# Running the FFN's first matmul four blocks ahead of its second instead of one, in an eight-core transformer layer

## The chip, the cores and the metric

The kernel runs on one Trainium2 chip with 8 cores. Each core takes one batch element (4096 tokens of width 1024) and all weights, and works alone; the cores exchange nothing. The metric is the device time of one launch in microseconds (us), that of the slowest core.

## The reference, cut to what matters

One post-layernorm transformer layer in float32: causal attention with 16 heads of 64, then a feed-forward network (FFN) with 4096 hidden units. Both are followed by a residual add and a layernorm.

```python
def _L0_ffn_ref(x, w1, b1, w2, b2):
    h = jax.nn.gelu(jnp.einsum('bse,eh->bsh', x, w1) + b1, approximate=False)
    return jnp.einsum('bsh,he->bse', h, w2) + b2

x = L0_attn_hidden_states                       # (8, 4096, 1024)
x = _layernorm(x + _L0_attn_ref(x, ...), axis=-1)
x = _layernorm(x + _L0_ffn_ref(x, ...), axis=-1)
```

## The kernel before, in words

Every operation is entered once, in program order, with `sch.add` (or `sp_dma`, `gp_dma` for transfers) and the operations that it depends on. Each engine then runs its own operations strictly in the order in which they were entered, and waits on a semaphore for each dependency on another engine. So the order of the `sch.add` calls is the order of the work, per engine. A `sch.barrier()` separates three stages. Stage A is attention by pairs of heads, stage B is the output projection with the first layernorm, and stage C is the FFN with the second layernorm. The change lies in stage C, which begins at 2704 us of the profiled execution.

Stage C keeps w1 and w2 in SBUF as bf16. w1 was loaded in stage B; w2 comes in at the start of stage C in 32 transfers, one per block of hidden units, issued from GpSimd's queue with at most two under way. The tokens are cut into 16 groups of 256 (`NTGC`, `TGC`). For each group the kernel goes over 32 blocks of 128 hidden units, `hc`:

- F1 (line 1153): 8 matmuls of 128x256, which multiply w1 by the transposed tokens `x2Tt` into one PSUM bank. Banks 0 and 1 take turns.
- gelu (line 1175) on ScalarE, from that bank to a bf16 tile `htile`, of which there are two (`hb = hc % 2`).
- F2 (line 1190): 4 matmuls of 128x512, `htile` by w2, added up over all 32 blocks in banks 2 to 5. In the last block 4 more matmuls (line 1200) add the bias and close the sums.

F1 of block hc+1 is entered between the gelu and the F2 of block hc, so TensorE computes F1 one block ahead. At a group's end there is no next block in the loop (`f1_next = None`). What follows the last F2 is the group's layernorm, called the tail here: four VectorE adds of the residual, out of banks 2 to 5 (line 1219), two squares on ScalarE with a running sum (line 1236), small VectorE statistics (lines 1249 to 1285), Ln and Exp on ScalarE (1299, 1308), a small VectorE product (1317), two ScalarE passes that write the output (1329), and the store. Ln and gelu sit in different activation tables, so ScalarE loads a table ahead of Ln and another ahead of the next gelu. ScalarE's order is gelu 31 of group g, the tail of g, gelu 0 of group g+1.

The loads of a group (`x2Tt` in 8 transfers and the residual rows `x2t` in one, both double-buffered, SyncE's queue, line 229) are entered at the group's top. The `x2Tt` load waits until the last F2 of the group two earlier is done, the `x2t` load until that group's tail has read its buffer.

Of the kernel before, what the change touches and what calls it, by code (L numbers as in the profile page):

```python
# [7 lines left out]
F32 = mybir.dt.float32  # L8
BF16 = mybir.dt.bfloat16
AF = mybir.ActivationFunctionType  # L10
# [3 lines left out]
D = 1024  # L14
FF = 4096
NPAIR = 8
TGA = 512
TGC = 256
# [85 lines left out]
def build_nc(S=4096, debug_taps=False):  # L104
# [3 lines left out]
    NTGC = S // TGC  # L108

    nc = bass.Bass("TRN2", target_bir_lowering=False)  # L110
# [16 lines left out]
    r_d = nc.dram_tensor("r_s", [2, 1024], F32, kind="Internal").ap()  # L127
    if debug_taps:
        qkv_tap = nc.dram_tensor("qkv_tap", [3, 128, S], BF16, kind="ExternalOutput").ap()

    idf_d = nc.inline_tensor(np.eye(128, dtype=np.float32), "idf")
    idb_d = nc.inline_tensor(
# [14 lines left out]
    rowbf = nc.alloc_sbuf_tensor("rowbf", [128, 5632], BF16).ap()  # L147
# [5 lines left out]
    b1f = nc.alloc_sbuf_tensor("b1f", [128, 32], F32).ap()  # L153
# [10 lines left out]
    def bf(off, n):  # L164
        assert off + n <= AR_COLS, f"arena overflow {off}+{n} > {AR_COLS}"
        return AR[:, off : off + n]

    def f32v(off, n):
        assert off % 2 == 0 and off + 2 * n <= AR_COLS, f"arena f32 ovf {off}"
        return AR[:, off : off + 2 * n].bitcast(F32)  # L170
# [28 lines left out]
    C_w1 = 0  # L199
    C_w2 = C_w1 + 8 * FF  # L200
    C_h = C_w2 + 32 * 1024
    C_x2T = C_h + 2 * TGC
    C_x2 = C_x2T + 2 * 8 * TGC
    C_out = C_x2 + 2 * 4096
    C_scr = C_out + 2 * 4096
# [5 lines left out]
    def bank(i):  # L211
        return PS[:, 512 * i : 512 * i + 512]
# [4 lines left out]
    sch = Sched(nc)  # L217
    t = nc.tensor
    v = nc.vector
    sc = nc.scalar  # L220
# [3 lines left out]
    def sp_dma(stream, outs_ins, deps=(), tag=""):  # L224
        sem = sch._sem(stream)

        def em():
            for o, i in outs_ins:
                sp.dma_start(out=o, in_=i).then_inc(sem, 16)
        return sch.add("sp", em, deps, tag, n_dma=len(outs_ins), sem=stream)  # L230

    def gp_dma(stream, outs_ins, deps=(), tag=""):
        sem = sch._sem(stream)

        def em():
            for o, i in outs_ins:
                gp.dma_start(out=o, in_=i).then_inc(sem, 16)  # L237
        return sch.add("pool", em, deps, tag, n_dma=len(outs_ins), sem=stream)
# [39 lines left out]
    eb1 = sch.add("dve", lambda: v.tensor_copy(b1f, PS[0:128, 2048:2080]), (tb1,), "b1Tev")  # L278
# [307 lines left out]
    for tp_ in range(NTT // 2):  # L586
# [28 lines left out]
        ev = sch.add("dve", em_ev, (tr,), f"xTev{tp_}")  # L615
# [182 lines left out]
    w1sb = bf(B_w1, 8 * FF)  # L798
# [10 lines left out]
    for oc in range(8):  # L809
# [19 lines left out]
        ev = sch.add("dve", em_ev, (tr,), f"wpTev{oc}")  # L829
# [3 lines left out]
    w1_lds = []  # L833
# [19 lines left out]
    for g in range(NTG):  # L853
        sb_ = 48 * (g % 2)
# [22 lines left out]
        for tc in range(4):  # L877
            for oh in range(2):
                bki = (2 * tc + oh) % 2
# [23 lines left out]
                def em_y2(tc=tc, oh=oh, bki=bki, xtg=xtg, sb_=sb_, y2=y2):  # L903
# [9 lines left out]
                ev = sch.add(  # L913
                    "dve", em_y2, (mm, x_ld) + y2_readers_par[g % 2], f"y2{g}.{tc}.{oh}"
                )
# [103 lines left out]
        for tc in range(4):  # L1019
# [6 lines left out]
                    bias=stats[:, sb_ + 36 + tc : sb_ + 37 + tc],  # L1026
# [11 lines left out]
                    bias=stats[:, sb_ + 36 + tc : sb_ + 37 + tc],  # L1038
# [66 lines left out]
    w2sb = bf(C_w2, 32 * 1024)  # L1105
    sq_scrC = f32v(C_scr, 1024)
    w2_lds = []
# [6 lines left out]
        )  # L1114
        w2_lds.append(ld)

    h_user = [None, None]
    gelu_prev = [None, None]
    x2t_user = [None, None]
    x2_user = [(), ()]  # L1120
    out_store = [None, None]
    ffn2_bank_user = [None, None, None, None]
    prev_sqC = None
    for g in range(NTGC):
        gb = g % 2
        sb_ = 48 * gb
        x2Tt = bf(C_x2T + gb * 8 * TGC, 8 * TGC)
        x2t = f32v(C_x2 + gb * 4096, 2048)
        outt = f32v(C_out + gb * 4096, 2048)
        ld1 = sp_dma(  # L1130
            f"sa{g % 2}",
            [
                (x2Tt[:, TGC * fc : TGC * fc + TGC], x2T_d[fc][:, TGC * g : TGC * g + TGC])
                for fc in range(8)
# [1 line left out]
            (x2t_user[gb],),  # L1136
            f"cx2T{g}",
        )
        ld2 = sp_dma(
            f"sx{g % 2}",  # L1140
            [(
                x2t.rearrange("p (c f) -> p c f", c=2, f=1024),
                x2_d[TGC * g : TGC * g + TGC, :].rearrange("(c p) f -> p c f", p=128),
# [1 line left out]
            x2_user[gb],  # L1145
            f"cx2{g}",
        )
        def mk_f1(hc, x2Tt=x2Tt, g=g):
            hb = hc % 2
            def em_f1(hc=hc, hb=hb, x2Tt=x2Tt):  # L1150
                r = None
                for fc in range(8):
                    r = t.matmul(  # L1153
                        bank(hb)[:, 0:TGC],
                        w1sb[:, FF * fc + 128 * hc : FF * fc + 128 * hc + 128],
                        x2Tt[:, TGC * fc : TGC * fc + TGC],
                        start=(fc == 0),
                        stop=(fc == 7),
                    )
                return r  # L1160
            deps1 = [ld1, gelu_prev[hb]]
            if g == 0 and hc == 0:
                deps1 += w1_lds
            return sch.add("pe", em_f1, tuple(deps1), f"f1_{g}.{hc}")

        ffn2_first = True
        mm2 = None
        f1_next = mk_f1(0)
        for hc in range(32):
            hb = hc % 2  # L1170
            htile = bf(C_h + hb * TGC, TGC)
            mm1 = f1_next
            gl = sch.add(
                "act",
                lambda hc=hc, hb=hb, htile=htile: sc.activation(  # L1175
                    htile, bank(hb)[:, 0:TGC], AF.Gelu, bias=b1f[:, hc : hc + 1]
                ),
                (mm1, h_user[hb]) + ((eb1,) if g == 0 and hc == 0 else ()),
                f"gelu{g}.{hc}",
            )  # L1180
            gelu_prev[hb] = gl
            if hc < 31:
                f1_next = mk_f1(hc + 1)
            else:
                f1_next = None
            def em_f2(hc=hc, htile=htile, first=ffn2_first, last=(hc == 31)):
                r = None
                for tc in range(2):
                    for oh in range(2):
                        r = t.matmul(  # L1190
                            bank(2 + 2 * tc + oh),
                            htile[:, 128 * tc : 128 * tc + 128],
                            w2sb[:, 1024 * hc + 512 * oh : 1024 * hc + 512 * oh + 512],
                            start=first,
                            stop=False,
                        )
                if last:
                    for tc in range(2):
                        for oh in range(2):
                            r = t.matmul(  # L1200
                                bank(2 + 2 * tc + oh),
                                rowbf[0:1, 3072 : 3072 + 128],
                                rowbf[0:1, 4608 + 512 * oh : 4608 + 512 * oh + 512],
                                start=False,
                                stop=True,
                            )
                return r
            deps_f2 = [gl, w2_lds[hc]]
            if ffn2_first:
                deps_f2 += [d for d in ffn2_bank_user if d is not None]  # L1210
            mm2 = sch.add("pe", em_f2, tuple(deps_f2), f"f2_{g}.{hc}")
            h_user[hb] = mm2
            ffn2_first = False
        x2t_user[gb] = mm2
        ev_ops = []
        for tc in range(2):
            for oh in range(2):
                def em_y3(tc=tc, oh=oh, x2t=x2t, sb_=sb_):
                    return v.scalar_tensor_tensor(  # L1219
                        x2t[:, 1024 * tc + 512 * oh : 1024 * tc + 512 * oh + 512],  # L1220
                        bank(2 + 2 * tc + oh),
                        1.0,
                        x2t[:, 1024 * tc + 512 * oh : 1024 * tc + 512 * oh + 512],
                        ALU.mult,
                        ALU.add,
                        accum_out=stats[:, sb_ + 2 * tc + oh : sb_ + 2 * tc + oh + 1],
                    )
                ev = sch.add("dve", em_y3, (mm2, ld2), f"y3{g}.{tc}.{oh}")
                ffn2_bank_user[2 * tc + oh] = ev
                ev_ops.append(ev)  # L1230
        stat_ops = []
# [94 lines left out]
        for tc in range(2):  # L1326
# [6 lines left out]
                    bias=stats[:, sb_ + 36 + tc : sb_ + 37 + tc],  # L1333
# [4 lines left out]
            )  # L1338
            ap_ops.append(ap1)
        x2_user[gb] = tuple(ev_ops + sq_ops + ap_ops)  # L1340
        st = gp_dma(
            f"pa{g % 2}",
            [(
# [54 lines left out]
```

How the kernel before makes its waits and increments, by code:

```python
    def emit_engine(self, name, eng):  # L80
        sems = self.sems
        wm = {}
        for op in self.ops:
            if op.eng != name:
                continue
            for d in op.deps:
                if d.eng == "pe" and name == "pe":
                    continue
                v = d.val
                if wm.get(d.sem, 0) >= v:
                    continue
                eng.wait_ge(sems[d.sem], v)
                wm[d.sem] = v
            last = op.emit()
            if not op.is_dma:
                assert last is not None, f"op {op.tag} returned no instruction"
                last.then_inc(sems[op.sem], 1)
        if name == "pool":
            for sname, val in sorted(self.final.items()):
                if val > 0 and sname not in ("pe", "act", "dve"):
                    eng.wait_ge(sems[sname], val)
# [125 lines left out]
        def em():  # L227
            for o, i in outs_ins:
                sp.dma_start(out=o, in_=i).then_inc(sem, 16)
# [5 lines left out]
        def em():  # L235
            for o, i in outs_ins:
                gp.dma_start(out=o, in_=i).then_inc(sem, 16)
```

## Time and profile before

| what | value |
|---|---|
| time, median of 2 runs | 3853.24 us (3835.53 and 3870.95) |
| the profiled execution's own time | 3833.8 us |
| its span, slowest core (core 2) | 3832.3 us |
| spans of the 8 cores | 3810.2 to 3832.3 us |
| mean granted TensorE clock, every core | 0.886 to 0.892 |
| TensorE busy over the span | 2808.2 us (73%) |
| ScalarE busy over the span | 1722.7 us (45%) |
| first matmul of stage C | 2704.4 us |

The span is counted from the first to the last instruction of the core, and 1.5 us of the execution's time lie around it. TensorE is busy for three quarters of the span in the mean, but that is a mean of three stages with different limits, so the stage of the change has to be read by itself. "Granted clock" is the share of TensorE's 2.4 GHz that the chip let it have: rows show 1.00 or 0.50, and values between are means over a stretch that holds both. Some matmul records (a few per cent) are missing from the trace, so counts in it can be short by a few.

### The profile page before, as it was taken

How to read it: one execution, taken by the hardware profiler on the slowest of the kernel's cores; microseconds unless marked ns; L12 is line 12 of the kernel's file. 1: busy time of each engine (PE TensorE's matmuls, PEld its weight loads, DVE VectorE, ACT ScalarE, POOL GpSimd, SP SyncE). 2: the span in 40 equal slices, each digit the busy share in tenths (PEclk: the TensorE clock that was granted, in tenths of full speed). 3: DMA queues.
4: the chain of work that ended last, by engine and by line, in shares of the span. 5: the costliest groups of instructions: out<-in, count | busy, mean ns of one | idle time of the engine just before them, and what ended most of it. 6: DMA issues, size and time to landing. Idle time of an engine off the chain costs nothing.

```text
span 3832.3 us, 40822 instructions; the slowest of 8 cores (3810.2 to 3832.3 us)
## 1 busy us (share of the span) xinstructions
PE 2808.2 (73%) x14609; PEld 1235.5 (32%) x14609; DVE 1174.2 (31%) x2008; ACT 1722.7 (45%) x1969; POOL 337.7 (9%) x447
## 2 busy tenths in 40 slices
PE   5777667677668667677767675387678888788886
PEld 3421123121123121123221111132345555555554
DVE  3354353354353354353354343133000000000000
ACT  0036634736734736733736786145133333333333
POOL 1010100010100010100010111012200000000000
PEclk9889888989898988888979899688889989899898
DMA  5200000010100010100010000965720110101100
GB/s 78 34 9 9 25 6 12 6 28 6 28 6 12 6 28 6 28 6 12 6 28 6 23 12 13 189 224 198 149 60 28 34 50 28 56 28 34 50 28 23
DMA packets 71682, 154.55 MB, mean 40 GB/s; under 512 B 9760, under 2 KB 34496, under 8 KB 69440
## 3 DMA queue, kind: packets, MB, share of 16 engines
q0 software_dynamic: 34784, 100.96, 10.6%
q1 hardware_dynamic: 36704, 50.98, 4.6%
q8 instruction: 124, 2.03, 0.2%
q14 instruction: 70, 0.57, 0.1%
HBM read 134.88 MB, written 50.59 MB: 48 GB/s over the span
## 4 chain that ended last, share of the span: by engine, by line
PE 56%; ACT 14%; DVE 12%; DMA 9%; issue 8%; POOL 1%; DVEq 0%; ACTq 0%; SPq 0%; POOLq 0%
ACT arena L673 12%; PE ps L1190 11%; PE ps L1153 11%; PE ps L701 10%; PE ps L374 7%; PE ps L649 6%; PE ps L540 3%; PE ps L883 3%; DVE rowf L728 3%; DMA arena<-x 3%; DVE arena L682 2%; DMA arena<-w 2%; DVE rowf L727 2%; DMA arena<-wqkv 2%; PE ps L415 1%
## 5 line engine op out<-in xcount | busy, mean ns | idle before, releaser
L673 ACT ACTIVATE arena<-ps,cbt 128x1024 bf16<-128x1024 f32 x1152 | 1245.3, 1112 | 938.5 <-PE ps L649 932.0
L701 PE MATMUL ps<-arena 128*65 128x512 bf16 x2304 | 751.7, 410 | 327.5 <-DVE arena L682 157.3
L1190 PE MATMUL ps<-arena 128*128 128x512 bf16 x2048 | 539.0, 388 | 165.6 <-ACT arena L1175 146.7
L1153 PE MATMUL ps<-arena 128*128 128x256 bf16 x4096 | 543.5, 278 | 18.0 <-DMA arena<-x2T_s 18.0
L1175 ACT ACTIVATE arena<-ps,b1f 128x256 bf16<-128x256 f32 x512 | 240.5, 473 | 668.8 <-PE ps L1153 668.6
L649 PE MATMUL ps<-arena 64*128 64x512 bf16 x2304 | 474.5, 410 | 0.0
L1153 PEld LDWEIGHTS ps<-arena 128*128 128x128 bf16 x4096 | 406.3, 100 | 184.2 <-issue 33.8
L682 DVE TENSOR_TENSOR arena<-arena,masks_s 128x512 bf16<-128x512 bf16 x512 | 198.8, 430 | 639.2 <-ACT arena L673 638.7
L701 PEld LDWEIGHTS ps<-arena 128*65 128x65 bf16 x2304 | 170.5, 113 | 632.0 <-issue 621.5
L1219 DVE SCALAR_TENSOR_TENSOR arena<-ps,arena 128x512 f32<-128x512 f32 x64 | 40.4, 687 | 1026.5 <-PE ps L1200 1026.5
L1190 PEld LDWEIGHTS ps<-arena 128*128 128x128 bf16 x2048 | 199.8, 99 | 319.8 <-issue 191.8
L649 PEld LDWEIGHTS ps<-arena 64*128 64x128 bf16 x2304 | 111.1, 94 | 519.8 <-issue 519.7
L374 PE MATMUL ps<-arena 128*128 128x512 bf16 x1024 | 255.3, 394 | 23.2 <-DVE arena L609 11.8
L415 PE MATMUL ps<-arena,ones_bf 128*1 128x512 bf16 x128 | 57.9, 452 | 243.6 <-DVE arena L406 243.6
L727 DVE RECIPROCAL rowf<-arena 1x512 f32<-1x512 f32 x64 | 213.8, 3341 | 12.0 <-DVE arena L720 12.0
L728 DVE RECIPROCAL rowf<-arena 1x512 f32<-1x512 f32 x64 | 210.0, 3282 | 0.0
L883 PE MATMUL ps<-arena 128*128 128x512 bf16 x512 | 137.6, 417 | 61.0 <-DVE arena L904 60.1
L237 POOL DMA_DIRECT2D r_s<-rowf x64 | 34.7, 543 | 1658.5 <-DVE rowf L728 943.9
L395 DVE CAST arena<-ps 128x512 bf16<-128x512 f32 x128 | 88.5, 691 | 299.8 <-PE ps L381 299.7
L540 PE MATMUL ps<-arena 128*128 128x256 bf16 x1024 | 144.5, 288 | 14.6 <-DVE arena L568 13.6
L374 PEld LDWEIGHTS ps<-arena 128*128 128x128 bf16 x1024 | 93.4, 100 | 157.4 <-issue 73.6
L928 ACT ACTIVATE arena<-arena 128x1024 f32<-128x1024 f32 x32 | 33.8, 1056 | 189.0 <-PE ps L1066 107.6
(92 smaller groups left out, 1446.0 us busy)
## 6 DMA issues: line engine op xcount, KB each, us to landing
rb<-r_s POOLq DMA_DIRECT2D x64, 256.0 KB, 3.5
arena<-x SPq DMA_DIRECT2D x8, 2048.0 KB, 9.9
x_s<-arena POOLq DMA_DIRECT2D x8, 2048.0 KB, 7.4
arena<-x_s SPq DMA_DIRECT2D x16, 1024.0 KB, 6.2
out<-arena POOLq DMA_DIRECT2D x16, 1024.0 KB, 8.3
arena<-x POOLq DMA_DIRECT2D x16, 512.0 KB, 7.5
attn_s<-arena POOLq DMA_DIRECT2D x8, 1024.0 KB, 5.2
arena<-attn_s SPq DMA_DIRECT2D x64, 128.0 KB, 10.7
```

What stands on the lines that cost most here:

```text
L374: r = t.matmul(bank(bki), wT[:, 128 * fc : 128 * fc + 128], xTb[:, S * fc + TGA * g : S * fc + TGA * g + TGA], start=(fc == 0), stop=False,)
L540: r = t.matmul(bank(bki)[:, 0:256], xTb[:, S * fc + 128 * a : S * fc + 128 * a + 128], wvg[:, 256 * fc : 256 * fc + 256], start=(fc == 0), ...
L649: r = t.matmul(PS[:, 1024 * ub + 512 * hh : 1024 * ub + 512 * hh + 512], k2[64 * hh : 64 * hh + 64, 128 * j : 128 * j + 128], q2[64 * hh : ...
L673: return sc.activation(Pb, quad, AF.Exp, bias=cbcol, scale=0.125)
L682: r = v.tensor_tensor(Pb[:, 512 * hh : 512 * hh + 512], Pb[:, 512 * hh : 512 * hh + 512], masks[:, 512 * mi : 512 * mi + 512], ALU.mult,)
L701: r = t.matmul(PS[0:65, 3072 + 512 * hh : 3584 + 512 * hh], va[:, 65 * (NKT * hh + j) : 65 * (NKT * hh + j) + 65], Pb[:, 512 * hh : 512 * ...
L727: v.reciprocal(rowf[0:1, 0:512], attnU[64:65, 0:512]),
L728: v.reciprocal(rowf[0:1, 512:1024], attnU[64:65, 512:1024]),
L883: r = t.matmul(bank(bki), atg[:, TGA * fc + 128 * tc : TGA * fc + 128 * tc + 128], wpT[:, 1024 * fc + 512 * oh : 1024 * fc + 512 * oh + 51 ...
L1153: r = t.matmul(bank(hb)[:, 0:TGC], w1sb[:, FF * fc + 128 * hc : FF * fc + 128 * hc + 128], x2Tt[:, TGC * fc : TGC * fc + TGC], start=(fc = ...
L1175: lambda hc=hc, hb=hb, htile=htile: sc.activation(htile, bank(hb)[:, 0:TGC], AF.Gelu, bias=b1f[:, hc : hc + 1]),
L1190: r = t.matmul(bank(2 + 2 * tc + oh), htile[:, 128 * tc : 128 * tc + 128], w2sb[:, 1024 * hc + 512 * oh : 1024 * hc + 512 * oh + 512], sta ...
```

## The change

F1 now runs four blocks ahead, over the group boundaries too. The loop over groups and the loop over blocks become one loop over 512 blocks `ui`. F1 of blocks 0 to 3 is entered ahead of the loop, and each turn enters gelu `ui`, F1 `ui+4` and F2 `ui`. F1 uses four PSUM banks (0, 1, 6, 7; 6 and 7 lay idle in stage C), and there are four `htile` buffers, so the later buffers of the arena move up by 512 columns. F1 `ui+4` waits for gelu `ui`, which frees its bank, and gelu `ui` waits for F2 `ui-4`. The tail is entered after the F2 of a group's last block as before. The loads of groups 0 and 1 are entered ahead of the loop, and those of group g+2 after the tail of group g; the `x2Tt` load now waits for F1 of group g's last block instead of its last F2. The number and the kind of the operations stay the same.

```diff
-    C_x2T = C_h + 2 * TGC
+    C_x2T = C_h + 4 * TGC
...
-    h_user = [None, None]
-    gelu_prev = [None, None]
+    F1BANKS = [0, 1, 6, 7]
+    h_user = [None, None, None, None]
+    gelu_bank = [None, None, None, None]
...
-            deps1 = [ld1, gelu_prev[hb]]
-            if g == 0 and hc == 0:
-                deps1 += w1_lds
-            return sch.add("pe", em_f1, tuple(deps1), f"f1_{g}.{hc}")
...
-        f1_next = mk_f1(0)
-        for hc in range(32):
-            hb = hc % 2
...
-            if hc < 31:
-                f1_next = mk_f1(hc + 1)
-            else:
-                f1_next = None
...
+    def mk_f1c(ui):
+        g, hc = ui // 32, ui % 32
+        gb = g % 2
+        x2Tt = bf(C_x2T + gb * 8 * TGC, 8 * TGC)
+        hb = ui % 4
+        bki = F1BANKS[hb]
...
+        deps1 = [ld1s[g], gelu_bank[hb]]
+        if ui == 0:
+            deps1 += w1_lds
+        return sch.add("pe", em_f1, tuple(deps1), f"f1_{g}.{hc}")
+
+    c_loads(0)
+    c_loads(1)
+    f1q = [mk_f1c(0), mk_f1c(1), mk_f1c(2), mk_f1c(3)]
+    NUC = NTGC * 32
+    for ui in range(NUC):
...
+            (mm1, h_user[hb]) + ((eb1,) if ui == 0 else ()),
+            f"gelu{g}.{hc}",
+        )
+        gelu_bank[hb] = gl
+        f1q.pop(0)
+        if ui + 4 < NUC:
+            f1q.append(mk_f1c(ui + 4))
...
+        mm2 = sch.add("pe", em_f2, tuple(deps_f2), f"f2_{g}.{hc}")
+        h_user[hb] = mm2
+        if hc != 31:
+            continue
+        x2t_user[gb] = mm1
...
+        c_loads(g + 2)
```

TensorE's order at a group boundary before (here between groups 14 and 15). L1153 is F1, L1190 is F2, L1200 the bias matmuls of the last block; in brackets the semaphores that a row waits for (`sem_act` is ScalarE, `sem_dve` VectorE, `sem_sa1` the `x2Tt` load).

```order
L1153 MATMUL ps<-arena 128x256 x8
L1190 MATMUL ps<-arena 128x512 [waits sem_act]
L1190 MATMUL ps<-arena 128x512 x3
L1190 MATMUL ps<-arena 128x512 [waits sem_act]
L1190 MATMUL ps<-arena 128x512 x3
L1200 MATMUL ps<-rowbf 128x512 x4
L1153 MATMUL ps<-arena 128x256 [waits sem_sa1]
L1153 MATMUL ps<-arena 128x256 x15
L1190 MATMUL ps<-arena 128x512 [waits sem_act,sem_dve]
L1190 MATMUL ps<-arena 128x512 x3
```

Behind the bias matmuls stand 16 F1 matmuls, the blocks 0 and 1 of the next group, which wait for no ScalarE work; the first row that waits for ScalarE is the F2 behind them.

The same place after the change. L1163 is F1, L1205 is F2, L1215 the bias matmuls.

```order
L1163 MATMUL ps<-arena 128x256 [waits sem_act]
L1163 MATMUL ps<-arena 128x256 x7
L1205 MATMUL ps<-arena 128x512 x4
L1215 MATMUL ps<-rowbf 128x512 x4
L1163 MATMUL ps<-arena 128x256 [waits sem_act]
L1163 MATMUL ps<-arena 128x256 x7
L1205 MATMUL ps<-arena 128x512 [waits sem_dve]
L1205 MATMUL ps<-arena 128x512 x3
```

The F1 behind the bias matmuls is block 4 of the next group, and its first matmul waits for ScalarE: for gelu 0 of that group. Blocks 0 to 3 were computed ahead of the last F2.

TensorE's order at the end of the program after the change: what follows the last F1.

```order
L1163 MATMUL ps<-arena 128x256 x7
L1205 MATMUL ps<-arena 128x512 x4
L1205 MATMUL ps<-arena 128x512 [waits sem_act]
L1205 MATMUL ps<-arena 128x512 x3
L1205 MATMUL ps<-arena 128x512 [waits sem_act]
L1205 MATMUL ps<-arena 128x512 x3
L1205 MATMUL ps<-arena 128x512 [waits sem_act]
L1205 MATMUL ps<-arena 128x512 x3
L1205 MATMUL ps<-arena 128x512 [waits sem_act]
L1205 MATMUL ps<-arena 128x512 x3
L1215 MATMUL ps<-rowbf 128x512 x4
```

Five F2 blocks stand in a row, since F1 has run out four blocks earlier; before, two did.

## Rows read from the trace of the kernel before

**Rows 1.** Windows: PE, PEld, DVE, ACT, POOL busy (count), clock, DMA share, GB/s.
```profile
3604.00:3673.00 69.00, 59.27 (x396) 38.75 (x394) 3.78 (x17) 22.75 (x43) 0.70 (x1) 0.93 0.13 39
3626.00:3640.00 14.00, 14.00 (x98) 9.46 (x97) 0.00 (x0) 3.86 (x9) 0.00 (x0) 1.00 0.00 1
...
3607.35:3612.35 5.00, 1.76 (x16) 1.33 (x14) 3.62 (x16) 2.74 (x5) 0.00 (x0) 0.98 0.40 105
...
2764.00:2784.00 20.00, 14.36 (x90) 8.04 (x89) 0.00 (x0) 3.52 (x8) 3.17 (x6) 1.00 0.73 103
```

**Rows 2.** Waits from 2600 us on: us in total, times, longest us.
```profile
PE ps L1190 <- ACT arena L1175: 146.7, 15, 10.3
...
PE ps L1190 <- DMA arena<-w: 18.8, 24, 1.6
```

**Rows 3.** Timeline inside a group: start us, us, engine, line, operation.
```profile
3601.78 1.04 PE L1153 MATMUL ps<-arena 128*128 128x256 bf16 x8
...
3602.66 1.03 PE L1190 MATMUL ps<-arena 128*128 128x512 bf16 x4
3602.92 0.47 ACT L1175 ACTIVATE arena<-ps,b1f 128x256 bf16<-128x256 f32 x1 [1.26 <-PE ps L1153]
...
3603.52 1.04 PE L1153 MATMUL ps<-arena 128*128 128x256 bf16 x8
```

**Rows 4.** Timeline at the boundary between groups 12 and 13.
```profile
3606.23 1.03 PE L1200 MATMUL ps<-rowbf 1*128 1x512 bf16 x4
...
3607.19 1.92 PE L1153 MATMUL ps<-arena 128*128 128x256 bf16 x16
3607.35 3.64 SPq L229 DMA_DIRECT2D arena<-x2T_s  x8
3607.44 0.69 DVE L1219 SCALAR_TENSOR_TENSOR arena<-ps,arena 128x512 f32<-128x512 f32 x1 [61.75 <-PE ps L1200]
...
3616.50 1.28 ACT L1175 ACT_TABLE_LOAD   x1
...
3617.79 0.84 ACT L1175 ACTIVATE arena<-ps,b1f 128x256 bf16<-128x256 f32 x2
...
3618.84 1.86 PE L1190 MATMUL ps<-arena 128*128 128x512 bf16 x4 [9.72 <-ACT arena L1175]
```

**Rows 5.** The chain that ended last, stage C: start us, us, engine, line.
```profile
2797.57 1.86 PE ps L1190 x4
...
2866.81 1.86 PE ps L1190 x4
...
2935.62 1.87 PE ps L1190 x4
...
3674.56 0.98 PE ps L1200 x4
3680.17 1.28 ACT L1299
...
3742.83 0.98 PE ps L1200 x4
3748.44 1.28 ACT L1299
```

**Rows 6.** Windows from TensorE's restart to the rise of its clock, and behind.
```profile
2797.60:2803.10 5.50, 5.50 (x19) 2.61 (x20) 0.00 (x0) 0.47 (x1) 0.00 (x0) 0.50 0.97 345
...
2866.90:2871.40 4.50, 4.50 (x15) 2.08 (x15) 0.00 (x0) 0.47 (x1) 0.00 (x0) 0.50 0.99 322
...
2935.70:2939.60 3.90, 3.90 (x14) 1.99 (x14) 0.00 (x0) 0.31 (x1) 0.00 (x0) 0.50 0.96 321
...
3618.90:3622.30 3.40, 3.40 (x13) 1.76 (x14) 0.00 (x0) 0.00 (x0) 0.00 (x0) 0.50 0.96 298
3622.40:3623.00 0.60, 0.60 (x5) 0.25 (x3) 0.00 (x0) 0.47 (x1) 0.00 (x0) 1.00 1.06 437
```

**Rows 7.** Timeline at the last block of group 0.
```profile
2783.43 1.02 PE L1190 MATMUL ps<-arena 128*128 128x512 bf16 x4 [1.60 <-DMA arena<-w]
```

More of the change, by code:

```diff
@@ L129, in build_nc @@
         qkv_tap = nc.dram_tensor("qkv_tap", [3, 128, S], BF16, kind="ExternalOutput").ap()
+        y3_tap = nc.dram_tensor("y3_tap", [S, D], F32, kind="ExternalOutput").ap()
     idf_d = nc.inline_tensor(np.eye(128, dtype=np.float32), "idf")
@@ L1123, in build_nc, with c_loads @@
     prev_sqC = None
-    for g in range(NTGC):
+    ld1s = [None] * (NTGC + 1)
+    ld2s = [None] * (NTGC + 1)
+    def c_loads(g):
+        if g >= NTGC:
+            return
         gb = g % 2
-        sb_ = 48 * gb
         x2Tt = bf(C_x2T + gb * 8 * TGC, 8 * TGC)
         x2t = f32v(C_x2 + gb * 4096, 2048)
-        outt = f32v(C_out + gb * 4096, 2048)
-        ld1 = sp_dma(
-            f"sa{g % 2}",
+        ld1s[g] = sp_dma(
+            f"sa{gb}",
             [
@@ L1138, in build_nc @@
         )
-        ld2 = sp_dma(
-            f"sx{g % 2}",
+        ld2s[g] = sp_dma(
+            f"sx{gb}",
             [(
@@ L1147, in build_nc @@
         )
-        def mk_f1(hc, x2Tt=x2Tt, g=g):
-            hb = hc % 2
-            def em_f1(hc=hc, hb=hb, x2Tt=x2Tt):
-                r = None
-                for fc in range(8):
-                    r = t.matmul(
[L1154 to L1158, printed above, removed]
-                    )
-                return r
-            deps1 = [ld1, gelu_prev[hb]]
-            if g == 0 and hc == 0:
-                deps1 += w1_lds
-            return sch.add("pe", em_f1, tuple(deps1), f"f1_{g}.{hc}")
@@ L1166, in build_nc, with em_f1 @@
-        ffn2_first = True
-        mm2 = None
-        f1_next = mk_f1(0)
-        for hc in range(32):
[L1170 to L1181, printed above, removed]
-            if hc < 31:
-                f1_next = mk_f1(hc + 1)
-            else:
-                f1_next = None
-            def em_f2(hc=hc, htile=htile, first=ffn2_first, last=(hc == 31)):
-                r = None
+    def mk_f1c(ui):
[4 more added lines that the diff above has]
+        bki = F1BANKS[hb]
+        def em_f1(hc=hc, bki=bki, x2Tt=x2Tt):
+            r = None
+            for fc in range(8):
+                r = t.matmul(
+                    bank(bki)[:, 0:TGC],
+                    w1sb[:, FF * fc + 128 * hc : FF * fc + 128 * hc + 128],
+                    x2Tt[:, TGC * fc : TGC * fc + TGC],
+                    start=(fc == 0),
+                    stop=(fc == 7),
+                )
+            return r
+        deps1 = [ld1s[g], gelu_bank[hb]]
+        if ui == 0:
+            deps1 += w1_lds
+        return sch.add("pe", em_f1, tuple(deps1), f"f1_{g}.{hc}")
@@ new lines, in build_nc, with em_f2 @@
+    c_loads(0)
[3 more added lines that the diff above has]
+    for ui in range(NUC):
+        g, hc = ui // 32, ui % 32
+        gb = g % 2
+        x2t = f32v(C_x2 + gb * 4096, 2048)
+        outt = f32v(C_out + gb * 4096, 2048)
+        sb_ = 48 * gb
+        hb = ui % 4
+        htile = bf(C_h + hb * TGC, TGC)
+        mm1 = f1q[0]
+        gl = sch.add(
+            "act",
+            lambda hc=hc, hb=hb, htile=htile: sc.activation(
+                htile, bank(F1BANKS[hb])[:, 0:TGC], AF.Gelu, bias=b1f[:, hc : hc + 1]
+            ),
+            (mm1, h_user[hb]) + ((eb1,) if ui == 0 else ()),
+            f"gelu{g}.{hc}",
+        )
+        gelu_bank[hb] = gl
+        f1q.pop(0)
+        if ui + 4 < NUC:
+            f1q.append(mk_f1c(ui + 4))
+        def em_f2(hc=hc, htile=htile, first=(hc == 0), last=(hc == 31)):
+            r = None
+            for tc in range(2):
+                for oh in range(2):
+                    r = t.matmul(
+                        bank(2 + 2 * tc + oh),
+                        htile[:, 128 * tc : 128 * tc + 128],
+                        w2sb[:, 1024 * hc + 512 * oh : 1024 * hc + 512 * oh + 512],
+                        start=first,
+                        stop=False,
+                    )
+            if last:
@@ L1191, in em_f2 @@
                             bank(2 + 2 * tc + oh),
[L1192 to L1195, printed above, removed]
-                        )
[L1197 to L1214, printed above, removed]
+                            rowbf[0:1, 3072 : 3072 + 128],
+                            rowbf[0:1, 4608 + 512 * oh : 4608 + 512 * oh + 512],
+                            start=False,
+                            stop=True,
+                        )
+            return r
+        deps_f2 = [gl, w2_lds[hc]]
+        if hc == 0:
+            deps_f2 += [d for d in ffn2_bank_user if d is not None]
+        mm2 = sch.add("pe", em_f2, tuple(deps_f2), f"f2_{g}.{hc}")
[3 more added lines that the diff above has]
+        x2t_user[gb] = mm1
         ev_ops = []
@@ L1227, in em_y3 @@
                     )
-                ev = sch.add("dve", em_y3, (mm2, ld2), f"y3{g}.{tc}.{oh}")
+                ev = sch.add("dve", em_y3, (mm2, ld2s[g]), f"y3{g}.{tc}.{oh}")
                 ffn2_bank_user[2 * tc + oh] = ev
@@ L1340, in build_nc @@
         x2_user[gb] = tuple(ev_ops + sq_ops + ap_ops)
+        if debug_taps:
+            gp_dma(
+                "pbias",
+                [(
+                    y3_tap[TGC * g : TGC * g + TGC, :].rearrange("(c p) f -> p c f", p=128),
+                    x2t.rearrange("p (c f) -> p c f", c=2, f=1024),
+                )],
+                tuple(ev_ops),
+                f"y3tap{g}",
+            )
+        c_loads(g + 2)
         st = gp_dma(
```

## The prediction

> **What bounds the kernel now.** I read the cores first: all eight stand at spans within 0.6% and at the same mean clock, so one core speaks for all. Then I read the stretch in which the changed code runs, and in it the windows, the waits, the timeline of one block and of one boundary, and the chain that ended last.
>
> Inside a group TensorE never stops. A window of 14 us in the middle shows 14.00 us of matmul at a granted clock of 1.00, the upper of the two levels, 2.4 GHz [rows 1]. The timeline shows one block: F1 starts at 3601.78, F2 at 3602.66 (0.88 us later), the next F1 at 3603.52. A block takes 1.74 us, half of it F1 and half F2, so one F1 is 0.87 us [rows 3]. The gelu of a block takes 0.47 us and starts while the F2 of the block before is running; that leaves it about half a microsecond to spare even one block ahead. The waits confirm it: F2 waited for a gelu 15 times, not 512 times, and those 15 add up to 146.7 us, 9.8 us each [rows 2]. There are 15 boundaries between 16 groups. So the loop is bound by TensorE's own stream, and the only waits for ScalarE are at the boundaries.
>
> At a boundary the reader is to see this [rows 4]. The bias matmuls begin at 3606.23 and end at about 3607.2. F1 of the next group's blocks 0 and 1 starts at 3607.19 and is over at 3609.1. Meanwhile the tail starts on VectorE at 3607.44; its last piece on ScalarE, a table load, begins at 3616.50, the gelus follow at 3617.79, and TensorE restarts with F2 at 3618.84. From the last F2 to the restart it is 11.6 us. This length is set by VectorE and ScalarE alone, and two F1 blocks hide 1.74 us of it. In the chain of the span's end, boundary follows boundary at 3742.83 - 3674.56 = 68.27 us [rows 5].
>
> **The change part by part.** The operations are the same, so every term is one of position.
>
> *F1 four ahead inside the group.* It gives the gelus three more blocks of slack. The loop has no such wait to lose (TensorE 14.00 of 14.00 us), so this is worth 0. The bounds: nothing to gain, since TensorE's share is full; nothing to lose, since the number of semaphore waits per block stays one. The wait now stands at F1 instead of F2, and it is for a gelu done blocks ago.
>
> *The boundary.* ScalarE's order is as before: gelu 31, tail, gelu 0. The tail still begins with the end of the bias matmuls, so gelu 0 still comes 11 to 12 us behind them. What changes is what TensorE has left to do. Blocks 0 to 3 of the next group are done already, ahead of the last F2, where TensorE was busy anyway. The next row, F1 of block 4, waits for gelu 0, because it needs the bank that this gelu frees. TensorE stands still for the whole 11.6 us instead of 9.7. The work isn't lost but moved out of the hole into the busy part: between two last F2s there are 32 F1 either way, of which before 2 lay in the hole and now none. That is 2 x 0.87 = 1.74 us more for each of 14 stretches. In the fifteenth, the last group, only 28 F1 are left, against 30 exposed before: 1.74 us less. Sum: 13 x 1.74 = **+22.6 us**.
>
> *The start.* Group 0 must do 36 F1 instead of 32 before its last F2. It is held back by w2: F2 waited 24 times for those loads, 18.8 us [rows 2], and its last F2 still waited 1.60 us [rows 7]. Four F1 (3.5 us) fit into these waits, F1 of block 35 before the last F2 itself too (0.87 of the 1.60). 0 us while the loads are the bound; if that cover were gone, +3.5 us. Nothing is gained either, since the loads depend on nothing of this.
>
> *The loads on SyncE's queue.* Every `x2Tt` and `x2t` load is entered in the same order as before; only the `x2Tt` load is released some 5 us earlier. In later groups this puts it beside a full TensorE and an idle DMA. In group 0 it falls among the last w2 loads, where the 16 DMA engines are 0.73 busy. Its own work is 0.40 x 5 = 2.0 us of all engines [rows 1]. Some goes into the free quarter: between 0 and 2.0, I take **+1.0 us**. The two queues keep their order, and nothing else is issued from SyncE.
>
> *The clock behind the hole.* TensorE restarts at the lower level, 1.2 GHz. Four F2 matmuls take 1.7 us there against 0.87, so each cold microsecond costs about half a microsecond. The cold stretch isn't fixed. It was 5.6 us behind the first boundary (restart at 2797.57, rise at 2803.1 to 2803.2), then 4.6 and 4.1, and at the boundary of the twelfth group 3.5 (3618.84 to 3622.3) [rows 5, 6]. It crept into a rest position together with the 68.27 us rhythm, and stayed there. A rhythm 1.74 us longer need not rest at the same place, and the stretch may be anything that was seen. Before, the 15 of them sum to about 15 x 3.5 + 2.1 + 1.1 + 0.6 = 56.3 us. I take the mean of the three unsettled ones, 4.8 us, for all 15: 72 us, so 15.7 us more, at a half **+7.8 us**. The ends are 3.5 everywhere (-1.9 us) and 5.6 everywhere (+14 us).
>
> The Trainium skill, "TensorE: Matmul & The Clock Gate", Part 1, says that what is issued cold is a budget of time and not a number of matmuls, and that it varies with the moment of the restart. The rows agree that it varies, 3.5 to 5.6 us. By its rule this term has either sign; without it the sum would be 23.6 us.
>
> Sum: 22.6 + 0 + 1.0 + 7.8 = +31.4 us, or 0.8%. On the profiled execution's own 3833.8 us (span 3832.3 and 1.5 around it) this gives 3865.2 us. The two timed runs of before are 3835.53 and 3870.95, median 3853.24. Two of the three executions known lie at the low end, which is where I put the forecast; a little of the upper one goes in: **3867 us**.
>
> **The rivals.**
>
> *A, moved work only.* The clock settles again at 3.5 us, the rest stands: 22.6 + 1.0 - 1.9 = +21.7, so 3855.5 us. For it: before, the stretch did settle. Against: it settled only by meeting one rhythm. Chance 0.20.
>
> *B, long cold stretches.* The restart falls at the worst moment each time and TensorE stays at the lower level for twice 3.5 us: 15 x 7 - 56.3 = 48.7, at a half +24; with 23.6 that is +48, so 3881 us. For it: the row of 5.6 us is on this way. Against: none so long was seen. Chance 0.13.
>
> *C, not slower.* The boundary itself shortens, because the 8 `x2Tt` transfers no longer run beside the VectorE adds and the squares (3607.35 for 3.64 us, [rows 4]). If this slowed the tail, its removal pays at each of 15 boundaries. It decides from 31.4 / 15 = 2.1 us off the 11.6; with 2.5 us off the result is 31.4 - 37.5 = -6, so 3828 us. Against it speaks the chain: from bias matmuls to the Ln's table load it takes 5.61 us at 3674.56, where the load of group 15 runs, and 5.61 us at 3742.83, where no load is left to issue [rows 5]. Chance 0.05.
>
> *D, slower by more than 2%.* The upper clock is not held through a group. At a granted 0.90 for the 54.6 us of matmul between holes (68.27 - 11.6 - 2 of cold loss), 15 groups cost 15 x 54.6 x (1/0.90 - 1) = 91 us more; with 31.4 that is 3956 us. It decides from a level of about 0.95. Against: 1.00 in the loop on the row read, and the change makes TensorE's work less dense, not more. Chance 0.04.
> The Trainium skill, same page and part, states a current limit of 13/16 of the clock when three or more cores of a die run dense matmuls. No row of this stage shows such a level; by its figure this case would cost about 190 us.
>
> **How the numbers follow.** Forecast 0.58, A 0.20, B 0.13, C 0.05, D 0.04. The range runs from 3843 (between C and A, for an execution a little quick) to 3903 (B with half of the 35 us that the two runs of before lie apart, and a forecast on top of the upper run, 3871 + 31). It leaves out most of C and all of D. Two per cent is 77 us, about what a measurement of this kernel can tell from no change. The forecast, A, B and nearly all of C lie within it. Faster by over 2% would need 7 us off each 11.6 us hole: 0.02. Slower by over 2% is D: 0.04. Within: 0.94.
>
> **What would show the steps right or wrong.** The wait of TensorE for ScalarE at the boundaries should stand at the F1 line, 15 times, 11.5 to 12 us each, 175 us in total instead of 147. No F1 should lie between the bias matmuls and that wait. The distance between boundaries should be 70 us or more instead of 68.27, and the last one shorter (under 68.5). The distance from the bias matmuls to the Ln's table load should stay at 5.6 us. Block time inside a group: 1.74 us. The windows behind the restarts should show 0.50 for 3.5 to 5.6 us, not the same each time. Group 0's last F2 should come at 2783 to 2786 us. I am wrong if the hole shrinks below 9.7 us, if the loop shows a granted clock under 1.00, or if the boundaries still come every 68.3 us.

## The result, and the profile after

The changed kernel takes 1.0048 times the time of the one before, with a 95% interval of 1.0033 to 1.0063: some 18 us slower (13 to 24). Executions in which one die (four of the eight cores) ran at a lower granted clock than the other are left out of that ratio, and such dies out of every span below, while the medians over all executions (3839.68 us over 42 of before, 3906.97 us over 43 of the changed kernel) contain them and can't be compared. The profiled execution took 3858.98 us, with a span of 3857.5 us on its slowest core, against 3833.8 and 3832.3 before: 25.2 us more.

The slowest core is another one in the two profiles, and the cores reach stage C at different moments. So I read stage C by itself and on the same cores. From the first bias matmuls to the last (the end of group 0 to the end of group 15) it took 1025.0 to 1027.1 us on the eight cores before, median 1026.3, and takes 1046.0 to 1048.3 us now, median 1046.35: **+20.0 us**, and 19.6 to 22.2 us on the single cores. Group 0 (first F1 to the first bias matmuls) took 81.7 us in the mean of the eight before and takes 83.0 now, and the single cores spread over 5 us, so its +1.3 us is not told from nothing.

The waits from 2600 us on in the changed kernel (us in total, times, longest us). L1163 is F1, L1191 the gelu, L1215 the bias matmuls:

```profile
ACT arena L1191 <- PE ps L1205: 611.7, 448, 3.9
...
PE ps L1163 <- ACT arena L1191: 168.2, 15, 11.5
```

The wait of [rows 2], 146.7 us at F2, has gone to the F1 line: still 15 times, but 168.2 us. The reader is to see that no new kind of wait has come up on TensorE: the same wait is 21.5 us longer, 1.43 us at each boundary. The first row is ScalarE's own. Inside a group a gelu now waits for the F2 four blocks back, which frees its tile, and that costs nothing, since ScalarE has time to spare there.

The boundary between groups 13 and 14, timeline of the slowest core:

```profile
3698.78 1.03 PE L1205 MATMUL ps<-arena 128*128 128x512 bf16 x4
...
3699.74 1.03 PE L1215 MATMUL ps<-rowbf 1*128 1x512 bf16 x4
3700.94 0.69 DVE L1235 SCALAR_TENSOR_TENSOR arena<-ps,arena 128x512 f32<-128x512 f32 x1 [64.00 <-PE ps L1215]
...
3710.01 1.28 ACT L1191 ACT_TABLE_LOAD   x1
...
3711.30 1.57 ACT L1191 ACTIVATE arena<-ps,b1f 128x256 bf16<-128x256 f32 x4
...
3711.92 1.86 PE L1163 MATMUL ps<-arena 128*128 128x256 bf16 x8 [11.15 <-ACT arena L1191]
```

Against [rows 4], the two F1 blocks behind the bias matmuls are gone, and TensorE stands still from the bias matmuls on. Four gelus now follow each other at once (x4), since their F1 were done long before; nothing needs them that early. Two things are unlike the forecast's picture. The restart follows the first gelu's start by 0.62 us, where before it followed by 1.05 (3617.79 to 3618.84 in [rows 4]). And the distances between boundaries alternate. The chain that ended last on core 2, the core shown ahead of the prediction:

```profile
3401.13 0.98 PE ps L1215 x4
3406.74 1.28 ACT L1315
3470.55 0.98 PE ps L1215 x4
3476.15 1.28 ACT L1315
3541.07 0.98 PE ps L1215 x4
3546.68 1.28 ACT L1315
3610.49 0.98 PE ps L1215 x4
```

The distances are 69.42, 70.52 and 69.42 us, where before they were 68.27 [rows 5]; the mean of a pair is 69.97. The last distance, in front of the last group's end, is shorter, 67.03 us on this core. The piece from the bias matmuls to Ln's table load is 5.60 to 5.61 us, as before. Inside a group nothing changed:

```profile
3720.00:3760.00 40.00, 40.00 (x278) 27.05 (x277) 0.00 (x0) 10.91 (x23) 0.00 (x0) 1.00 0.00 1
```

That window shows 40.00 us of matmul in 40.00 us, at a granted clock of 1.00. The alternation comes with the cold stretch behind the restart (windows of the slowest core; the restarts are at 3711.92 and 3781.34):

```profile
3712.00:3715.10 3.10, 3.10 (x12) 1.64 (x12) 0.00 (x0) 0.87 (x3) 0.00 (x0) 0.50 0.94 279
3715.20:3715.80 0.60, 0.60 (x7) 0.52 (x6) 0.00 (x0) 0.32 (x1) 0.00 (x0) 1.00 1.00 396
3781.40:3786.80 5.40, 5.40 (x21) 2.98 (x22) 0.00 (x0) 1.36 (x4) 0.00 (x0) 0.50 0.44 181
3786.90:3787.50 0.60, 0.60 (x5) 0.24 (x4) 0.00 (x0) 0.00 (x0) 0.00 (x0) 1.00 0.00 0
```

TensorE is at 1.2 GHz for 3.2 us behind one restart and for 5.5 us behind the next, in turns, where before it had come to rest at 3.5 us [rows 6].

### The profile page after: what moved, and what is told of

The parts are those of the page before. It is cut to its first block, busy times and chain, and to the rows that moved or that the text cites. A ratio compares the mean times of both kernels' runs of the same rounds, so it can differ in the third digit from the quotient of the medians.

```text
span 3857.5 us, 41330 instructions; the slowest of 8 cores (3830.2 to 3857.5 us)
## 1 busy us (share of the span) xinstructions
PE 2819.2 (73%) x14609; PEld 1242.9 (32%) x14609; DVE 1174.2 (30%) x2008; ACT 1720.8 (45%) x1969; POOL 337.5 (9%) x447
## 4 chain that ended last, share of the span: by engine, by line
PE 56%; ACT 14%; DVE 11%; DMA 9%; issue 8%; POOL 1%; DVEq 0%; ACTq 0%; POOLq 0%; SPq 0%
ACT arena L674 12%; PE ps L1163 11%; PE ps L1205 11%; PE ps L702 10%; PE ps L375 6%; PE ps L650 6%; PE ps L541 3%; PE ps L884 3%; DVE rowf L729 3%; DMA arena<-x 3%; DVE arena L683 2%; DMA arena<-w 2%; DVE rowf L728 2%; DMA arena<-wqkv 2%; PE ps L416 1%
## 5 line engine op out<-in xcount | busy, mean ns | idle before, releaser
L1163 PE MATMUL ps<-arena 128*128 128x256 bf16 x4096 | 553.2, 280 | 184.3 <-ACT arena L1191 168.2
L1205 PE MATMUL ps<-arena 128*128 128x512 bf16 x2048 | 540.4, 388 | 18.1 <-DMA arena<-w 18.1
L1163 PEld LDWEIGHTS ps<-arena 128*128 128x128 bf16 x4096 | 409.6, 100 | 356.7 <-issue 200.3
L1191 ACT ACTIVATE arena<-ps,b1f 128x256 bf16<-128x256 f32 x512 | 238.0, 475 | 613.7 <-PE ps L1205 611.7
L1205 PEld LDWEIGHTS ps<-arena 128*128 128x128 bf16 x2048 | 203.1, 100 | 164.8 <-issue 34.1
L541 PE MATMUL ps<-arena 128*128 128x256 bf16 x1024 | 144.0, 287 | 14.7 <-DVE arena L569 13.6
```

Source lines behind the costliest of these rows:

```text
L541: r = t.matmul(bank(bki)[:, 0:256], xTb[:, S * fc + 128 * a : S * fc + 128 * a + 128], wvg[:, 256 * fc : 256 * fc + 256], start=(fc == 0), ...
L1163: r = t.matmul(bank(bki)[:, 0:TGC], w1sb[:, FF * fc + 128 * hc : FF * fc + 128 * hc + 128], x2Tt[:, TGC * fc : TGC * fc + TGC], start=(fc ...
L1191: lambda hc=hc, hb=hb, htile=htile: sc.activation(htile, bank(F1BANKS[hb])[:, 0:TGC], AF.Gelu, bias=b1f[:, hc : hc + 1]),
L1205: r = t.matmul(bank(2 + 2 * tc + oh), htile[:, 128 * tc : 128 * tc + 128], w2sb[:, 1024 * hc + 512 * oh : 1024 * hc + 512 * oh + 512], sta ...
```

## The experiments

The theory is that the loss is F1 work that left the hole: a block of F1 behind the bias matmuls costs nothing, ahead of them 0.87 us. This is theory 1 of the expectations below. Its rivals are that four-ahead costs something in itself (theory 2), and that the earlier `x2Tt` load disturbs (theory 3). All spans below are from the first to the last bias matmuls, the median over the cores.

**hold4: all four in the hole.** F1 still runs four ahead, but none of the next group's blocks is entered ahead of the last F2.

```diff
-        if ui + 4 < NUC:
+        if ui + 4 < NUC and hc < 28 + 0:
             f1q.append(mk_f1c(ui + 4))
...
+        if hc == 31 and ui + 4 < NUC:
+            for uj in range(ui + 1 + 0, ui + 5):
+                f1q.append(mk_f1c(uj))
```

> The changed kernel, but no F1 of the next group may be entered ahead of a group's last F2: blocks 0 to 3 of the next group all stand behind the bias matmuls. Theory 1 (the loss is the F1 work that left the hole, 0.87 us per F1 block and boundary): between the first and the last bias matmuls 30 F1 fewer are exposed than in the kernel before, so 26 us less than its 1026 us, about 1000, and about 6 us less still if the restart with F1 stays 0.43 us quicker; the time is 25 to 33 us under before, ratio 0.992 to 0.994. Theory 2 (running F1 four ahead with four banks costs time in itself, inside the groups): the block time is over 1.74 us and the run stays near the changed kernel, 1046 us or a little less. Theory 3 (the x2T load that is released earlier disturbs): no gain here either, since the load is released as in the changed kernel.

Measured: ratio to before 0.9914 (0.9895 to 0.9933), a shade below what was expected, and a span of 998.3 us, that is 28.0 us under before and 48 us under the changed kernel. The timeline at a boundary:

```profile
3390.25 1.03 PE L1215 MATMUL ps<-rowbf 1*128 1x512 bf16 x4
3391.22 3.67 PE L1163 MATMUL ps<-arena 128*128 128x256 bf16 x32
...
3402.43 1.87 PE L1163 MATMUL ps<-arena 128*128 128x256 bf16 x8 [7.55 <-ACT arena L1191]
```

32 F1 matmuls (3.67 us) run behind the bias matmuls; the restart comes 12.2 us behind the start of the bias matmuls as in the changed kernel, and the wait shrinks to 7.6 us. The loss is in where the four F1 stand. Depth and banks are the same as in the changed kernel, which rules out theory 2, and so is the release of the load, so theory 3 has no part in these 48 us.

**hold2: two in the hole, as before.** The same edit with `28 + 2` and `ui + 1 + 2`.

> The changed kernel, but only blocks 0 and 1 of the next group are entered ahead of a group's last F2; 2 and 3 stand behind the bias matmuls, so that two F1 blocks lie in the hole as in the kernel before. Theory 1: 448 F1 blocks exposed against 450, so 1.7 us less than before's 1026, and 6 us less still for the quicker restart, 1018 to 1025 us; ratio to before 0.997 to 1.000. Theory 2: stays at the changed kernel's 1046 us.

Measured: ratio 0.9986 (0.9973 to 1.0000), span 1024.6 us, 1.7 us under before. With two blocks in the hole the four-ahead kernel is as fast as the one-ahead kernel, within the interval. So, with the tail whole, depth gives nothing and takes nothing that these runs can tell. The three placements, with 0, 2 and 4 blocks in the hole, give 1046.35, 1024.6 and 998.3 us: 22 and 26 us less. In groups 1 to 14 they leave 32, 30 and 28 F1 blocks outside the hole, in the last group 28 each. So every step hides 28 blocks more, by 0.87 us a block 24.4 us for each step and 49 for both, and 48 was measured.

**late_load: the old release of the load.**

```diff
-        x2t_user[gb] = mm1
+        x2t_user[gb] = mm2
```

> The changed kernel, but the x2T load waits for the group's last F2 as in the kernel before. Theory 1: the span between the first and the last bias matmuls stays at 1046 us, within 1 us; the wait at the boundary stays at 11.5 us; group 0 up to 1 us shorter, which the spread of the cores (80.7 to 85.2 us) hides. Theory 3 (the early load costs): 5 us or more off the 1046.

Measured: span 1046.35 us, the same to a tenth, and a stop at the boundary of 11.5 us at most and 11.2 in the mean, as in the changed kernel. The moved load costs nothing between groups. Group 0 took 80.5 to 84.6 us on the eight cores here, in the same spread; the 1.0 us that the forecast gave it is neither shown nor refuted.

**hold2_f2first: TensorE restarts with F2.** In hold2, F2 of block 0 is entered ahead of F1 of block 4.

```diff
-        if ui + 4 < NUC and hc < 28 + 2:
+        if ui + 4 < NUC and hc < 28 + 2 and (hc != 0 or g == 0):
             f1q.append(mk_f1c(ui + 4))
...
+        if hc == 0 and g > 0:
+            f1q.append(mk_f1c(ui + 4))
```

> As hold2, but at block 0 of a group F2 is entered ahead of F1 of block 4, so that TensorE restarts with F2, as in the kernel before. If the 0.43 us by which the changed kernel restarts sooner after the first gelu belongs to the kind of operation that restarts (F2, with its weights from the gelu's tile and two semaphores to wait for, against F1), the restart comes 12.67 us behind the bias matmuls here as in before, against 12.24 in hold2 and in the changed kernel, and the span is about 6 us over hold2's. If it belongs to the four banks or the depth, it is 12.24 here too.

**hold2_f2first_1wait: the same F2 with one semaphore to wait for.** The last F1 in the hole also waits for VectorE's adds, so that F2 needs no wait for them.

```diff
+            f1q.append(mk_f1c(ui + 3))
+            f1q.append(mk_f1c(ui + 4, tuple(ev_ops)))
```

> hold2_f2first, but the last F1 in the hole also waits for VectorE's adds, so that the F2 that restarts TensorE has the semaphore of ScalarE alone to wait for. If the 0.43 us later restart with F2 comes from waiting for two semaphores, the restart comes 12.3 us behind the bias matmuls; if from F2 itself, 12.7 us as in hold2_f2first. The span stays at 1024 to 1025 us either way, since hold2 and hold2_f2first had the same rhythm of 68.26 us in spite of their different restarts.

The spans of these two runs are those of cores 4 to 7. I read the same core, core 5, in three runs. The gelus behind the hole and the restart, first in hold2:

```profile
3333.30 1.57 ACT L1191 ACTIVATE arena<-ps,b1f 128x256 bf16<-128x256 f32 x4
3333.92 1.86 PE L1163 MATMUL ps<-arena 128*128 128x256 bf16 x8 [9.30 <-ACT arena L1191]
```

In hold2_f2first:

```profile
3328.24 1.57 ACT L1191 ACTIVATE arena<-ps,b1f 128x256 bf16<-128x256 f32 x4
3329.28 1.87 PE L1205 MATMUL ps<-arena 128*128 128x512 bf16 x4 [9.74 <-ACT arena L1191]
```

In hold2_f2first_1wait:

```profile
3275.09 1.57 ACT L1191 ACTIVATE arena<-ps,b1f 128x256 bf16<-128x256 f32 x4
3275.71 1.86 PE L1205 MATMUL ps<-arena 128*128 128x512 bf16 x4 [7.26 <-ACT arena L1191]
```

From the gelu's start to the restart it is 0.62 us with F1 and one semaphore, 1.04 with F2 and two, 0.62 with F2 and one. So the 0.42 us belong to the second semaphore, although it (VectorE's) had long been up, and not to the kind of matmul. The kernel enters the wait for ScalarE ahead of the one for VectorE; the other order was not tried.

The span is 1024.6 us in hold2_f2first and 1023.8 in the third. For the third 1024 to 1025 was expected. For hold2_f2first it was a miss: some 6 us over hold2 were expected for the later restart, and the two spans are equal. Both have boundaries 68.26 us apart. The windows behind the restart, first of hold2 and then of hold2_f2first, show where the difference went:

```profile
3333.95:3338.30 4.35, 4.35 (x17) 2.43 (x18) 0.00 (x0) 1.40 (x4) 0.00 (x0) 0.50 0.92 283
3338.35:3338.80 0.45, 0.45 (x5) 0.39 (x4) 0.00 (x0) 0.00 (x0) 0.00 (x0) 1.00 1.04 428
3329.30:3332.70 3.40, 3.40 (x13) 1.81 (x14) 0.00 (x0) 0.51 (x2) 0.00 (x0) 0.50 0.83 295
3332.85:3333.30 0.45, 0.45 (x7) 0.40 (x5) 0.00 (x0) 0.35 (x1) 0.00 (x0) 1.00 1.04 428
```

The cold stretch is 4.4 us in hold2 against 3.5 in hold2_f2first. hold2 restarts 0.43 us sooner and stays at half speed 0.9 us longer, which costs about as much as was won.

**split_tail_hold4: the tail out of the gelus' way.** If the hole is made by ScalarE's order, it should go when that order is changed. hold4, and the group's tail is entered in three pieces among the next group's blocks: the squares ahead of gelu 2, Ln and Exp ahead of gelu 6, the output passes, store and loads ahead of gelu 10.

```diff
+        while pend and pend[0][0] <= ui:
+            pend.pop(0)[1]()
...
+        pend += [(ui + 1 + 2, tail_sq), (ui + 1 + 6, tail_ln), (ui + 1 + 10, tail_ap)]
```

> hold4 (four F1 blocks behind the bias matmuls), and the tail of a group is entered later on ScalarE and in three pieces among the next group's gelus: the squares ahead of gelu 2, Ln and Exp ahead of gelu 6, the two output passes ahead of gelu 10. Theory 1 says the hole is set by ScalarE's order, not by TensorE's: gelu 0 of the next group no longer stands behind the tail, so the hole closes, the lower clock behind it goes too, and what is left is 512 blocks of 1.74 us. Span from the first to the last bias matmuls 15 x 56.5 = 848 us plus at most 2 us per boundary, 848 to 880 instead of 1026; time 3660 to 3700 us, ratio 0.955 to 0.965. A rival, that VectorE's adds out of the F2 banks (2.8 us) and the table loads bind as soon as the order is changed: 930 us or more, ratio 0.975 or more.

Measured: the profiled execution took 3666.76 us and another 3669.47, against 3838 to 3843 us of before, too few for an interval. So the kernel was run again.

> The kernel of split_tail_hold4 once more, for an interval. Its group rhythm was 56.64 us on the settled stretch against 68.27 before, 15 times 11.6 us; so 3665 to 3670 us against 3836 to 3842 and a ratio of 0.953 to 0.957.

Measured: ratio 0.9553, 95% interval 0.9536 to 0.9570, 4.5% under before. The span, from the first of the two runs, is 850.9 us, within the 848 to 880 of theory 1 and far under the 930 of its rival, VectorE's adds and the table loads as the next bound. The chain has TensorE's rows alone, 56.64 us from boundary to boundary, and a window over 13 groups shows no gap at all:

```profile
3134.24 0.96 PE ps L1218 x4
...
3190.88 0.96 PE ps L1218 x4
```

```profile
2850.00:3600.00 750.00, 750.00 (x5143) 500.60 (x5142) 52.91 (x238) 296.67 (x562) 9.19 (x13) 1.00 0.15 46
```

TensorE is busy for 750.00 of 750.00 us at a granted clock of 1.00. How much of this the lead of four blocks gives is seen in split_tail_1ahead below. The timeline behind a boundary (L1164 F1, L1208 F2, L1194 gelu):

```profile
3134.17 1.03 PE L1218 MATMUL ps<-rowbf 1*128 1x512 bf16 x4
3135.13 4.54 PE L1164 MATMUL ps<-arena 128*128 128x256 bf16 x40
...
3136.28 0.47 ACT L1194 ACTIVATE arena<-ps,b1f 128x256 bf16<-128x256 f32 x1 [4.92 <-PE ps L1164]
...
3139.51 1.03 PE L1208 MATMUL ps<-arena 128*128 128x512 bf16 x4
...
3142.86 1.28 ACT L1327 ACT_TABLE_LOAD   x1
...
3144.67 1.28 ACT L1194 ACT_TABLE_LOAD   x1
```

Five F1 blocks cover VectorE's adds out of the F2 banks. ScalarE leaves its gelus for Ln and Exp at 3142.86 and is back at 3145.95, and TensorE does not notice, since it has four blocks of F1 in hand.

**split_tail: the changed kernel's placement with the same split.** F1 across the boundary as in the change, pieces ahead of gelus 4, 8 and 12.

> The changed kernel as it is (F1 four ahead across the boundary), with the same three pieces of the tail ahead of gelus 4, 8 and 12 of the next group. Theory 1: four blocks of F1 ahead are now of use, since gelus 0 to 3 of the next group run ahead of the squares. Only F1 of block 4 covers VectorE's adds, so some 2 us stay open per boundary: span 848 + 15 x 2 = 878 us, within 865 to 900; ratio 0.96 to 0.97, slower than split_tail_hold4 by 10 to 30 us. If the early F1 is a loss in itself, this run stays near the time of the kernel before.

Measured: ratio 0.9629 (0.9611 to 0.9646), span 886.4 us, as expected, but 36 us over split_tail_hold4 where 10 to 30 were. What is left open is VectorE, in the waits of 2850 to 3600 us:

```profile
PE ps L1208 <- DVE stats L1270: 18.8, 10, 1.9
PE ps L1208 <- DVE stats L1283: 6.3, 3, 2.1
```

That is 25.1 us at 13 boundaries, 1.9 us at a time: F2 of the next group can't start until VectorE has emptied its banks, and here only one F1 stands in between, not five. At 15 boundaries these waits make some 28 of the 36 us. The clock takes about what is left: at 5 or 6 of the 15 boundaries it was at the lower level for 3.4 to 6.8 us, 17 to 20 us in sum on each core, where split_tail_hold4 has at most one such stretch, at the end of group 0.

**split_tail_1ahead: one block of lead.** As split_tail, with `ui + 1` in place of `ui + 4`.

> As split_tail, but F1 runs one block ahead (still over the boundary, with the four banks). With one block of lead, each piece on ScalarE of more than about 1 us makes TensorE wait: squares 2.5 us, Ln and Exp with their table loads about 3.4, output passes 2.4. Expected open per boundary: 2 for VectorE's adds and 1.5 + 2.4 + 1.4 for the pieces, 7 us, so a span of 848 + 15 x 7 = 953 us, within 920 to 980. If depth doesn't matter once the tail is split, it is within 10 us of split_tail.

Measured: 3734.02 us in the execution that was read; span 918 to 921 us on six cores and 902 to 904 on two, median 919.4. That is 33 us over split_tail and just under the 920 to 980 that were expected. TensorE's waits from 2850 to 3600 us on the slowest core:

```profile
PE ps L1208 <- DVE stats L1270: 24.4, 13, 1.9
PE ps L1208 <- ACT arena L1194: 10.4, 12, 1.1
```

VectorE's 1.9 us are as in split_tail. New is a wait for a gelu, 0.9 us in the mean at each boundary, so TensorE stands still 2.7 us at a boundary and not the 7 that were expected. This makes 13 of the 33 us. The other large part is the clock: over the same stretch the mean granted clock is 0.97 on the six cores and 0.99 on the two, and 0.99 on all eight of split_tail. On the six the clock fell behind 14 or 15 of the 15 boundaries, 48 to 51 us at the lower level in sum against 20 in split_tail. The two cores on which it fell at only 4 or 5 are 16 to 18 us over split_tail. So depth matters once the tail is split, and with the tail whole it did not (hold2), but less than half of the 33 us is the waits themselves, and some 5 us of them are not placed.

## Why the prediction was right

The forecast was +31.4 us, 0.8%, within 2%, and it was so: 1.0048. The way is right. The size was forecast at 31.4 us, and it is 20.0 between the first and the last bias matmuls and some 18 by the ratio. By its steps:

*F1 four ahead inside the group, 0.* Right. TensorE is full in the loop, and hold2 equals before within the interval. A reading in the working was off: the gelu of [rows 3] ends at 3603.39 and its F2 starts at about 3604.4, so one block of lead left it 1.0 us to spare, not half a microsecond; nothing hangs on it.

*The boundary, +22.6 us.* Right in kind and size. No F1 stands behind the bias matmuls, the 15 waits stand at the F1 line. hold2 and hold4 bear out the price of 0.87 us for each block that leaves the hole or goes in (48 us for 56 blocks). The wait was forecast at 11.5 to 12 us and 175 us in total; it is 11.2 in the mean, 11.5 at most, and 168.2, since the restart comes sooner than was read (below).

*The start and the loads, +1.0 us.* late_load gives 0 between groups; group 0 can't be told from the spread of the cores.

*The clock behind the hole, +7.8 us.* This is the term of the sum that was mis-sized. "The stretch may be anything that was seen" was right as a warning, but the mean of three unsettled stretches, 4.8 us, was too long. On core 2 the 15 stretches sum to 56.8 us before and 64.4 after, 4.3 each, since they fall into turns of 3.2 and 5.5. For the same reason the distance between boundaries stayed just under the 70 us that were to show the step right, 69.97 in the mean of a pair. What a cold microsecond costs is read from the distances in turns: 70.52 - 69.42 = 1.10 us for 2.26 us more of the lower level, 0.49 us each. So the longer stretches are +3.7 us, not +7.8.

*What the sum lacked.* The restart with one semaphore to wait for instead of two, 0.43 us sooner at 15 boundaries: -6.4 us (from the start of the bias matmuls to the restart, 190.0 us in sum before and 183.6 after, core 2). I had read the restart as fixed by the gelu alone, though the order rows showed F2 with two semaphores and F1 with one.

With these two terms core 2 comes out: 22.6 + 3.7 - 6.4 = 19.9 us, and its span went from 1026.6 to 1046.4. For hold4, with 66 us of cold stretch in the mean of its cores, the same sum is -26.1 + 0.49 x (66 - 56.8) - 6.5 = -28.1, and 28.0 was measured. This adds up what the records show; it doesn't price the two terms apart. hold2 and hold2_f2first differ in the restart alone, and the cold stretch took the whole of it back. What the changed kernel would take with the later restart was not run.

*The rivals.* A (moved work only, the clock at rest again) had 21.7 us, which lies nearer to the measured 18 to 20 than the forecast does, but by luck and not for its reason: the clock did not come to rest at 3.5 us, and the sooner restart made up for it. B is refuted, the stretch is 5.5 us at most in the settled rhythm. C is refuted by late_load and by the 5.61 us that did not move. D is refuted by the clock of 1.00 inside the groups.

## What to carry to other kernels

Ask what a wait hides before moving work away from it: running an engine further ahead takes free work out of a hole that another engine's order makes, at its full price. The hole has to be closed where it is made; with the tail entered in pieces among the next group's gelus and four F1 blocks left behind the boundary, the same lead of four blocks stands in a kernel that is 4.5% faster than before, and not 0.5% slower. Most of that is the split; with the split alone and a lead of one block the span was 107 us under before, with four blocks it was 140, and with four left behind the boundary 175.

## What the runs showed that I had not expected

A matmul that waits for two semaphores starts 0.42 us later behind the last of them than one that waits for one (1.04 us against 0.62 from the gelu's start), even when the other had been up for some 8 us. The runs don't tell where in TensorE's queue this is spent or whether the order of the two waits plays a part, and both cases were seen with the clock at the lower level only.

A periodic hole and the clock behind it can fall into step. With holes that TensorE restarts from cold, the distances settled at 68.27 us (before), 68.26 (hold2, hold2_f2first and hold2_f2first_1wait), or in turns at 69.42 and 70.52 (changed kernel) and at 66.01 and 67.11 (hold4). A gain or a loss of half a microsecond at the restart may then vanish in the cold stretch, so that small edits at such a boundary can't be priced one by one. What sets the moment of the rise was not tried apart.
